# A linear attention kernel: values folded behind the key product, keys scaled on another engine, new instruction orders

## What is computed

```
h = layernorm(x)
q = elu(h Wq + bq) + 1;  k = elu(h Wk + bk) + 1;  v = h Wv + bv      # 16 heads of 8 features
k = k / sqrt(sum over a head's 8 features of k*k + 1e-6)
attn = (q k^T) v, head by head, without softmax                      # = q (k^T v)
y = h + attn Wo + bo;  x1 = x + layernorm(y) * gamma + beta
n = layernorm(x1);  s = n . w_router
in each batch the 768 rows of largest s:  out = x1 + gelu(n W_block)
the other 256 rows:                       out = x1 + n
```

## Time and profile before

| | us |
|---|---|
| median of 3 runs (96.92 to 98.74) | 97.76 |
| the profiled execution, whole | 97.48 |
| its span, first to last instruction | 95.5 |

### The profile page before, as it was taken

How to read it: one execution, slowest core, us unless ns; L and a number is a source line. 1 busy time by engine, 2 the same in 40 slices (tenths; PEclk the granted TensorE clock), 3 DMA queues, 4 the chain that set the end, 5 groups by cost and what they waited for, 6 DMA issues and landing times.

```text
span 95.5 us, 2547 instructions
## 1 busy us (share of the span) xinstructions
PE 85.9 (90%) x870; PEld 74.5 (78%) x870; DVE 85.3 (89%) x252; ACT 67.3 (71%) x174; POOL 61.5 (64%) x114
## 2 busy tenths in 40 slices
PE   4997899899999999999999999999879999999500
PEld 1344559797979996997799999999779997969400
DVE  4328999999999999999999999999999999999750
ACT  5004299897997775668593788759988969698900
POOL 5154189999990185760975799998999898402400
PEclk9999999999999999999999999999999999999965
DMA  1999799999989970000000000000000006104386
GB/s 34 262 297 302 181 288 293 283 173 130 147 97 134 140 93 0 0 0 0 0 7 0 0 0 3 0 0 7 0 0 7 0 3 190 37 0 117 110 253 186
DMA packets 18114, 9.01 MB, mean 94 GB/s; under 512 B 819, under 2 KB 18102, under 8 KB 18102
## 3 DMA queue, kind: packets, MB, share of 16 engines
q1 hardware_dynamic: 12704, 6.23, 24.2%
q0 software_dynamic: 4160, 2.10, 19.9%
q10 hardware_dynamic: 1238, 0.53, 1.9%
HBM read 4.66 MB, written 2.10 MB: 71 GB/s over the span
## 4 chain that ended last, share of the span: by engine, by line
PE 48%; DVE 21%; POOL 12%; issue 5%; DMA 5%; ACT 2%; ACTq 2%; DVEq 1%
PE bank L1129 10%; PE bank L1204 6%; PE bank L1145 6%; PE bank L1120 5%; DMA x_sb<-in_L_attn_x_dram 5%; PE bank L1165 5%; PE bank L1164 5%; DVE norm_sb L722 4%; DVE bn L713 4%; POOL r L361 3%; DVE x_sb L874 3%; POOL x_sb L376 3%; DVE beats L856 2%; PE bank L1183 2%; PE bank L1224 2%
## 5 line engine op out<-in xcount | busy, mean ns | idle before, releaser
L1129 PE MATMUL bank<-w_c,hT 128*128 128x128 f32 x120 | 15.3, 276 | 0.0
L1129 PEld LDWEIGHTS bank<-w_c,hT 128*128 128x128 f32 x120 | 14.3, 192 | 0.9 <-ACT hT L466 0.7
L376 POOL TENSOR_TENSOR x_sb<-x_sb,xb_sb 128x512 f32<-128x512 f32 x8 | 10.5, 1324 | 5.7 <-ACT x_sb L537 5.4
L544 ACT ACTIVATE norm_sb<-xb_sb,shift,gain 128x128 f32<-128x128 f32 x32 | 13.1, 487 | 0.0
L1165 PE MATMUL bank<-back,hT 128*128 128x128 f32 x64 | 12.4, 275 | 0.0
L1164 PE MATMUL bank<-M_sb,qT 128*128 128x128 f32 x64 | 12.4, 275 | 0.0
L843 DVE TENSOR_SCALAR beats<-s_row,s_col 128x896 bf16<-128x896 f32 (+6 forms) x28 | 12.0, 477 | 0.0
L537 ACT ACTIVATE x_sb<-bank,r 128x128 f32<-128x128 f32 x32 | 9.4, 375 | 3.0 <-DVE s_col L823 2.9
L856 DVE SCALAR_TENSOR_TENSOR beats<-s_row,s_col,later 128x128 bf16<-128x128 f32 x32 | 10.0, 371 | 0.0
L1165 PEld LDWEIGHTS bank<-back,hT 128*128 128x128 f32 x64 | 9.7, 192 | 0.0
L1164 PEld LDWEIGHTS bank<-M_sb,qT 128*128 128x128 f32 x64 | 9.7, 192 | 0.0
(11 more groups left out here) (117 smaller groups left out, 212.7 us busy)
## 6 DMA issues: line engine op xcount, KB each, us to landing
xb_sb<-in_L_attn_x_dram SPq DMA_DIRECT2D x4, 512.0 KB, 6.8
xb_sb<-beta_sb POOLq DMA_DIRECT2D x4, 512.0 KB, 7.2
out_dram<-x_sb SPq DMA_DIRECT2D x7, 256.0 KB, 2.3
x_sb<-in_L_attn_x_dram SPq DMA_DIRECT2D x6, 256.0 KB, 5.7
x_sb<-in_L_attn_x_dram SPq DMA_DIRECT2D x2, 128.0 KB, 2.9
x_sb<-in_L_attn_x_dram ACTq DMA_DIRECT2D x1, 256.0 KB, 4.7
out_dram<-x_sb SPq DMA_DIRECT2D x1, 128.0 KB, 3.1
out_dram<-x_sb ACTq DMA_DIRECT2D x1, 128.0 KB, 3.1
```

The costliest lines, as they stand in the source:

```text
L376: nc.gpsimd.tensor_tensor(x_sb[:, a:a + TH], x_sb[:, a:a + TH], xb_sb[:, a:a + TH], ALU.add).then_inc(gelu_sums, 1)
L544: last = nc.scalar.activation(norm_sb[:, t], xb_sb[:, t], ACT.Identity, bias=shift3[:, t:t + 1], scale=gain3[:, t:t + 1])
L1129: last = nc.tensor.matmul(o[:, t * P:(t + 1) * P], hT[:, u, t * P:(t + 1) * P], w_c[:, vector * P:(vector + 1) * P], start=True, stop=True)
```

## The change

The values are never made. PE multiplies h (the rows in `norm_sb`) with the keys, h^T k, over a batch's eight tiles; ACT copies the 128x128 result (`copy_hk`), PE multiplies it once by Wv (`values`), and the head mask and Wo follow as before. `v_proj` and `scale_v` are gone. The keys themselves are now divided by their norms, in place in SBUF, by POOL (`scale_k`, eight times, with an inner pattern of eight equal norms). For the biases, feature 127 of h is overwritten by ones: only 127 columns are normalised, and as the features of h sum to zero, the projection weights are folded so that the lost feature is recovered (`less_last`, `to_last`), with the bias in their last row; `back` is folded likewise (`less_bo`, where bo arrives by its transfer), and `spread_bo` is gone. The keys keep a buffer for every half in place of a ring of six. The lists of all engines and the banks' uses are in a new order. Cut to its core (the rest of the lists is in the same manner; ACT's list, in which `normalise1(7)` stands just ahead of `copy_hk(0)`, most of PE's and the middle of DVE's, and `BANK_USES` are left out):

```diff
-    KRING = 6
...
+    KEYS_BY = 'PPPPPPPP'
...
-        k_sb = sb("k_sb", [P, KRING, TH, D])
+        k_sb = sb("k_sb", [P, U, TH, D])
         k2_sb = sb("k2_sb", [P, 2, TH * HEADS, DEPTH])
         k_ssq = sb("k_ssq", [P, 2, T * HEADS])
         k_seed = sb("k_seed", [P, 2, T * HEADS])
         k_tmp = sb("k_tmp", [P, 2, T * HEADS])
-        k_rnorm = sb("k_rnorm", [P, 2, T * HEADS])
-        v_sb = sb("v_sb", [P, KRING, TH, D])
+        k_rnorm = sb("k_rnorm", [P, B, T * HEADS])
+        hk_sb = sb("hk_sb", [P, B, P])
...
+        def scaled_keys(u):
+
+            a = TH * HEADS * (u % 2)
+            keys = k_sb[:, u].rearrange("p t (h e) -> p (t h) e", e=DEPTH)
+            return keys, keys, k_rnorm[:, u // 2, a:a + TH * HEADS].unsqueeze(2).to_broadcast([P, TH * HEADS, DEPTH])
...
             def first_masks():
                 nc.gpsimd.memset(minus_half[:], -0.5)
                 nc.gpsimd.memset(centre[:], -1.0 / D)
-                nc.gpsimd.memset(average[:], 1.0 / (LIFT * D))
+                nc.gpsimd.memset(to_last[:, 0:P - 1], 0.0)
+                nc.gpsimd.memset(to_last[:, P - 1:P], 1.0)
+                nc.gpsimd.memset(less_last[:, P - 1:P], 0.0)
                 link(nc.gpsimd.memset(ident[:], 0.0))
                 nc.gpsimd.affine_select(out=ident[:], in_=ident[:], compare_op=ALU.not_equal, fill=1.0, base=0,
                                         pattern=[[-1, P]], channel_multiplier=1)
-                nc.gpsimd.affine_select(out=centre[:], in_=centre[:], compare_op=ALU.not_equal, fill=1.0 - 1.0 / D, base=0,
-                                        pattern=[[-1, P]], channel_multiplier=1).then_inc(ident_set, 1)
+                link(nc.gpsimd.affine_select(out=centre[:], in_=centre[:], compare_op=ALU.not_equal, fill=1.0 - 1.0 / D, base=0,
+                                             pattern=[[-1, P]], channel_multiplier=1))
+                nc.gpsimd.affine_select(out=less_last[:, 0:P - 1], in_=ident[:, 0:P - 1], compare_op=ALU.is_ge, fill=-1.0,
+                                        base=P - 2, pattern=[[0, P - 1]], channel_multiplier=-1).then_inc(ident_set, 1)
 
             def masks():
+                nc.gpsimd.affine_select(out=less_bo[:, 0:P - 1], in_=ident[:, 0:P - 1], compare_op=ALU.is_ge, fill=-1.0,
+                                        base=P - 2, pattern=[[0, P - 1]], channel_multiplier=-1).then_inc(bo_cols, 1)
...
+            def scale_k(u):
+                pool.wait_ge(rnorm_done, u // 2 + 1)
+                out_keys, keys, norms = scaled_keys(u)
+                nc.gpsimd.tensor_tensor(out_keys, keys, norms, ALU.mult).then_inc(keys_pool, 1)
...
             roots1(2)
             shifts1(2)
             roots1(3)
+            roots1(4)
+            shifts1(4)
+            masks()
+            scale_k(0)
+            scale_k(1)
             add_beta(0)
-            roots1(4)
             add_beta(1)
-            masks()
             add_beta(2)
-            shifts1(4)
             add_beta(3)
+            scale_k(2)
+            scale_k(3)
             roots2(0)
             roots2(1)
             residual(0)
+            scale_k(4)
             roots3(0)
+            scale_k(5)
             affine3(0)
             roots2(2)
+            roots3(1)
             roots2(3)
-            roots3(1)
+            roots3(2)
             affine3(1)
-            roots3(2)
+            scale_k(6)
             roots2(4)
+            scale_k(7)
             roots2(5)
+            affine3(2)
             gelu_sum(0)
             roots3(3)
+            roots3(4)
+            roots3(5)
+            affine3(3)
             gelu_sum(1)
+            roots2(6)
             gelu_sum(2)
-            roots3(4)
-            affine3(2)
-            affine3(3)
             affine3(4)
-            roots3(5)
+            roots2(7)
             gelu_sum(3)
-            roots2(6)
-            roots2(7)
             gelu_sum(4)
-            gelu_sum(5)
             affine3(5)
             roots3(6)
+            gelu_sum(5)
             roots3(7)
+            gelu_sum(6)
             affine3(6)
             affine3(7)
-            gelu_sum(6)
             gelu_sum(7)
...
-                    last = nc.scalar.activation(norm_sb[:, t], x_sb[:, t], ACT.Identity, bias=shift1[:, t:t + 1],
+                    last = nc.scalar.activation(norm_sb[:, t, 0:P - 1], x_sb[:, t, 0:P - 1], ACT.Identity, bias=shift1[:, t:t + 1],
...
-                nc.scalar.activation(hT[:, u], bank_of(("h", u)), ACT.Identity, bias=lift[:, 0:1]).then_inc(hT_done, 1)
+                nc.scalar.copy(hT[:, u], bank_of(("h", u))).then_inc(hT_done, 1)
...
+            def copy_hk(b):
+                act.wait_ge(hk_full, b + 1)
+                nc.scalar.copy(hk_sb[:, b], bank_of(("M", b))[:, 0:P]).then_inc(hk_done, 1)
+
             def copy_M(b):
                 act.wait_ge(M_full, b + 1)
-                nc.scalar.copy(M_sb[:, b], bank_of(("M", b))[:, P:2 * P]).then_inc(M_done, 1)
+                nc.scalar.copy(M_sb[:, b], bank_of(("M", b))[:, 2 * P:3 * P]).then_inc(M_done, 1)
...
-                nc.vector.memset(lift[:], LIFT)
+                nc.vector.memset(norm_sb[:, :, P - 1:P], 1.0)
                 dve.wait_ge(bias_zero, 1)
                 nc.vector.memset(bias_rows[32:33, 0:2 * P], 1.0)
                 nc.vector.memset(minus1[:], -1.0).then_inc(dve_const, 1)
-
-            def spread_bo():
-
-                dve.wait_ge(bo_in, 16)
-                dve.wait_ge(ident_set, 1)
-                nc.vector.tensor_scalar(bo_diag[:], ident[:], LIFT * D, bo_col[:, 0:1], ALU.mult, ALU.add).then_inc(bo_set, 1)
...
-                    last = nc.vector.tensor_scalar(norm_sb[:, n], x_sb[:, n], mean[:, n:n + 1], r1[:, n:n + 1],
+                    last = nc.vector.tensor_scalar(norm_sb[:, n, 0:P - 1], x_sb[:, n, 0:P - 1], mean[:, n:n + 1], r1[:, n:n + 1],
...
-            def scale_v(u):
-                a = TH * HEADS * (u % 2)
-                dve.wait_ge(v_full, u + 1)
+            def scale_k(u):
                 dve.wait_ge(rnorm_done, u // 2 + 1)
-                if u >= KRING:
-                    dve.wait_ge(vk_full, (u - KRING) // 2 + 1)
-                nc.vector.tensor_tensor(v_sb[:, u % KRING].rearrange("p t (h e) -> p (t h) e", e=DEPTH),
-                                        bank_of(("v", u)).rearrange("p (n e) -> p n e", e=DEPTH),
-                                        k_rnorm[:, u // 2 % 2, a:a + TH * HEADS].unsqueeze(2)
-                                        .to_broadcast([P, TH * HEADS, DEPTH]), ALU.mult).then_inc(v_done, 1)
...
             constants()
             first_stats(0)
             first_stats(1)
+            bn_x(1)
             first_normalise(0)
-            bn_x(1)
             first_normalise(1)
             bn_x(2)
-            spread_bo()
             normalise1(1)
             bn_x(3)
             bn_x(4)
             bn_x(5)
             bn_x(6)
+            bn_x(7)
+            normalise1(2)
             k_half(0)
-            bn_x(7)
             k_half(1)
-            normalise1(2)
             normalise1(4)
-            q_half(0)
             normalise1(5)
             key_sums(0)
             key_sums(1)
+            q_half(0)
+            normalise1(6)
             k_half(2)
+            q_half(1)
+            key_norms(0)
             k_half(3)
-            normalise1(6)
-            key_norms(0)
+            key_sums(2)
             k_half(4)
-            scale_v(0)
-            scale_v(1)
             centre_wo()
-            key_sums(2)
-            q_half(1)
+            q_half(2)
             key_sums(3)
+            k_half(5)
             mask_vk(0)
...
+            merge(0)
+            compare_own(2, 0)
+            compare_own(2, 1)
             x1_stats(7)
-            compare(1, 5, 1)
-            compare(1, 6, 1)
+            score_cols(6, 0)
+            score_cols(6, 1)
             compare(2, 0, 1)
             compare(2, 1, 1)
-            compare_own(2, 0)
             compare(2, 2, 1)
             compare(2, 3, 1)
-            drop_last(0)
-            drop_first(0)
-            score_cols(6, 0)
-            merge(0)
-            score_cols(6, 1)
             compare(2, 4, 1)
-            merge(1)
             compare(2, 5, 1)
-            compare(2, 6, 1)
-            compare_own(2, 1)
+            drop_first(1)
+            drop_last(1)
             score_cols(7, 0)
             score_cols(7, 1)
-            drop_first(1)
-            drop_last(1)
             compare_own(3, 0)
+            compare(2, 6, 1)
             compare(3, 0, 1)
             compare(3, 1, 1)
-            merge(2)
             compare(3, 2, 1)
             compare(3, 3, 1)
             compare(3, 4, 1)
+            compare_own(3, 1)
             compare(3, 5, 1)
-            compare_own(3, 1)
             compare(3, 6, 1)
+            merge(1)
+            merge(2)
             merge(3)
             drop_first(2)
             drop_first(3)
             drop_last(2)
+            drop_last(3)
```

(57 more changed lines are left out.)

336 lines of the change are left out of this document (170 added, 166 removed), and 14 rows, old and new, of the table BANK_USES.

## The result

| | before | after |
|---|---|---|
| median of the runs | 97.53 us (4 runs, 96.92 to 98.74) | 101.66 us (4 runs, 101.41 to 102.74) |
| the profiled execution, its span | 97.48, 95.5 | 101.41, 99.6 |

The ratio is 1.047 (95% interval 1.036 to 1.058): the change made the kernel slower by 4.7%. The forecast was 96.8 us, with a range up to 100.8. The measured time lies outside it, and on the other side of before.

The account below looks back on a forecast made before the run. It took TensorE and VectorE, then GpSimd's queue, as bounds: `roots3(7)` ending at 80.1 us plus a 14.75 us tail gave a span of 94.85, with 1.98 around it 96.8 us; range 93.0 to 100.8.

Parts of the forecast that it names:

- not 6.2: TensorE's busy time: 7.1 us of value products removed, 0.9 us for `values` added, net 6.2 us less.
- With both handovers I take 0.8 us a batch: Way to M: one more ScalarE copy and one product, 0.8 us a batch, mostly hidden by a projection or transpose between.
- the odd length: VectorE's 24 normalisations writing 127 of 128 columns: taken as nothing, at most 1.6 us if speed fell to half.
- the 1.25 taken: GpSimd's eight `scale_k`: 1.25 us each, 10.0 us in all, priced from additions of the same size.
- the dear rival: GpSimd's `scale_k` slower through its grouped operand, 1.80 us each: 4.2 us more, 101.0 us; chance 0.22.
- The queue's end: GpSimd's list walked in order from about 24.0 us: `roots2(5)` ends at 55.5, `roots3(7)` at 80.1 us.
- Its last item: Last entry of GpSimd's sum to `roots2(5)`: `residual(0)` 1.3 us and two affine groups of 0.74, printed as 1.5.
- would reach `score_cols(7)` at about 75: VectorE, 5.0 us lighter, arrives at the last scores at about 75 us (80.90 before) and waits for GpSimd's last root.
- the disturbance between the two engines: GpSimd's small instructions stretched beside VectorE's comparisons after `roots2(5)`: 4.5 us, kept as before.
- The tail: From the end of `roots3(7)` through scores, comparisons, `merge(1)` and seven stores to the end: 14.75 us, 1.85 shorter than before.
- E + 1.7: E is the end of `roots3(7)`; from there, scores to a filled s_row were forecast at 1.7 us.
- The clock: Sign against the argument: TensorE's granted clock, 1.00 in both stages after 23.6 us, falling in the new gaps; no size given.

Follow-up runs that it names:

- e14: Changed kernel with five more products on zeros behind `fold_biases()`, to keep TensorE at work while it waits for x: 1.030 of before, span 98.4 us.
- e6: Changed kernel without the copy and the product with Wv between h^T k and its mask, so not the whole computation: 1.018 of before.
- e5: Kernel before with a copy and an identity product added between attention matrix and mask in all batches, and `attention_matrix(2)` ahead of `q_proj(6)`: 1.0445 of before.
- e8: Changed kernel without GpSimd's eight gelu sums (one column set to zero instead), so not the whole computation: 0.992 of before.
- e9: Kernel before without GpSimd's eight gelu sums (one column set to zero instead), so not the whole computation: 0.996 of before.
- e12: Kernel before with the added copy and product ahead of the mask in batch 3 alone, and `attention_matrix(2)` ahead of `q_proj(6)`: 1.014 of before.

## Why the prediction was wrong

- **TensorE.** The removal is there: the group of key and value products went from 15.3 to 7.4 us busy, against 1.6 us for `values`. Net it gave 2.4 us of busy time, not 6.2. The q projections took 9.0 us instead of 8.0, as part of them ran at half clock (8.0 again in e14); the rest is spread over groups that grew by 0.3 to 0.6 us each, and why is not shown.
- **"With both handovers I take 0.8 us a batch ... which hides most of it."** Too kind, in the changed orders by little (1.2 points in e6 against e14), in before's by much (4.4% in e5). No chain was followed from M to VectorE, where the mask now waits 1.6 us. Nor was the new order of the banks followed, which gives VectorE 1.41 us of idle time at 52 to 54 us.
- **VectorE.** `scale_v` is gone, and the odd length cost nothing (the 20 later normalisations: 349 ns, 401 before). The memset and the folding are nothing.
- **GpSimd.** `scale_k` took 1.08 us, less than the 1.25 taken, so groups of eight equal norms cost nothing and the dear rival was false. The reading of the Trainium skill, "GPSIMD Engine Reference", performance pitfalls, by which each group would be a command of its own and the instruction 5.4 us, is settled by the measurement: it is not so here. The queue's end stood nearly as walked, in part by luck: the eight `scale_k` took 8.5 us instead of 10.0, and waits of 2.3 us that were not in the walk filled it up. (Its last item, given as 1.5, is `residual(0)` 1.3 and the affine groups 1.5; the sum of 31.5 has both.) `roots2(5)` ended at 56.12, forecast 55.5, and `roots3(7)` at 82.65, forecast 80.1:

```profile
81.36 1.29 POOL L389 TENSOR_TENSOR r<-var,minus_half 128x4 f32<-128x4 f32 x1
```

- **The step that failed** is "VectorE, 5.0 us lighter, would reach `score_cols(7)` at about 75 ...: it waits". It came at 84.28, behind the root. A saving in busy time ahead of 54 us was carried over as time of arrival, but it had become idle time (4.8 us), and from 54.3 to 78.9 us VectorE had next to no idle time in either kernel. GpSimd was not the bound there; it had 4.6 us of idle time, 2.50 of it waiting for VectorE at 61 to 63.5. And of the disturbance between the two engines, seen in `gain`, only GpSimd's side was priced. The other side was put at nothing, and it is the dearer: 1 us of VectorE per gelu sum that falls on comparisons, 3.7 us in the changed kernel against 1.0 in before.
- **The tail.** From the end of `merge(1)`, 91.1, to the end of the span 8.45 us were forecast and 8.5 came. But `merge(1)` ended 8.5 us behind the root instead of 6.3: VectorE read the last scores 1.6 us behind it, and the last z waited 0.8 more for `dropped`, so s_row was full at E + 4.0 instead of E + 1.7.
- **The clock.** It was named as what could prove the argument wrong, but in the stages behind 23 us. It fell at 11 to 15, behind first transposes that had to wait for more of x. The moved `bn_x(1)` was counted as 0.3 us of VectorE.

The terms at their measured sizes, of a span longer by 4.1 us: start and clock 1.2 us (e14 against the changed kernel); collisions of the sums 2.7 us more than in before (e8, e9); the longer way to M 0.6 to 1.2 us (e6 against e14); the wait for the bank of `y_half(5)` 1.41 us of idle time just ahead of VectorE's full stretch, which no run tests by itself. The 4.3 us of work that VectorE no longer has before 54.3 us went into such waits. The terms overlap, as e12 shows, and do not add up exactly. In e5, comparisons, own comparisons and merges took 28.8 us, 1.0 more than in before, so about a quarter of its 4.4% is collision and the rest is waits and the start; how these two share it was not separated.
